# TensorE fill work behind the first group sums and behind the second piece's turn

## What is computed

```python
def ternary_quant(w_fp32, g=GROUP_SIZE):          # GROUP_SIZE = 64
    w = w_fp32.astype(jnp.bfloat16)
    w_g = w.reshape(-1, g)
    scale = jnp.clip(jnp.mean(jnp.abs(w_g), axis=-1, keepdims=True), 1e-08, None)
    q = jnp.clip(jnp.round(w_g / scale), -1, 1)
    w_hat = (q * scale).reshape(w.shape)
    return w + jax.lax.stop_gradient(w_hat - w)
...
x = x + 0.5 * _L0_ffn_ref(_layernorm(x, axis=-1), L0_ffn_w_gate_up, L0_ffn_w_proj)
x = x + _L0_attn_ref(_layernorm(x, axis=-1), L0_attn_w_qkv, L0_attn_w_proj, L0_attn_b_proj)
x = x + 0.5 * _L0_ffn_ref(_layernorm(x, axis=-1), L0_ffn_w_gate_up, L0_ffn_w_proj)
```

## Time and profile before

| | |
|---|---|
| median of 3 runs | 874.05 us |
| the profiled execution's own time | 873.84 us |
| span of its trace | 871.2 us |
| mean granted TensorE clock | 0.996 |
| VectorE busy | 511.7 us (59%) |
| ScalarE busy | 443.0 us (51%) |
| GpSimd busy | 71.5 us (8%) |

### The profile page before, as it was taken

One profiled execution on the slowest core, in us unless ns is written; L12 is line 12 of the kernel. 1 busy time (PEld: TensorE's weight loads), 2 busy tenths in 40 slices (PEclk: granted clock), 3 DMA queues, 4 the chain that ended last, 5 costly groups with the idle time before them and its releaser, 6 DMA issues. The chain is left out here.

```text
span 871.2 us, 13142 instructions
## 1 busy us (share of the span) xinstructions
PE 852.2 (98%) x4932; PEld 413.3 (47%) x4998; DVE 511.7 (59%) x979; ACT 443.0 (51%) x822; POOL 71.5 (8%) x114
## 2 busy tenths in 40 slices
PE   6999999999999989999999999999999999999998
PEld 5544444444444434464646464444444444444445
DVE  7999997824347566657696958433443443432332
ACT  7976667536435555556657463543444344334331
POOL 2211001200010010000000000000000000000000
PEclk9999999999999999999999999999999999999999
DMA  9999508996747679960505062163433343333236
GB/s 262 179 182 125 76 1 169 216 223 185 163 117 149 112 147 196 185 125 1 86 1 86 1 147 97 21 113 73 73 73 72 73 73 73 73 73 61 61 69 136
DMA packets 257486, 94.70 MB, mean 109 GB/s; under 512 B 242832, under 2 KB 245648, under 8 KB 256400
## 3 DMA queue, kind: packets, MB, share of 16 engines
q1 hardware_dynamic: 248448, 73.42, 45.2%
q0 software_dynamic: 5024, 13.11, 6.7%
q10 hardware_dynamic: 3952, 7.34, 2.6%
HBM read 29.62 MB, written 8.39 MB: 44 GB/s over the span
## 5 line engine op out<-in xcount | busy, mean ns | idle before, releaser
L1643 PE MATMUL proj_ps<-down_w,slots 128*128 128x512 bf16 x910 | 202.9, 379 | 1.1 <-issue 0.2
L1172 DVE SCALAR_TENSOR_TENSOR slots<-up_ps,silu 128x512 f32<-128x512 f32 x117 | 80.9, 691 | 179.8 <-PE up_ps L1629 134.2
L1629 PE MATMUL gate_ps<-gu_w,xT 128*128 128x512 bf16 (+1 forms) x762 | 173.1, 368 | 3.1 <-ACT silu L809 2.3
L1629 PE MATMUL up_ps<-gu_w,xT 128*128 128x512 bf16 (+1 forms) x759 | 171.3, 366 | 0.9
L1643 PEld LDWEIGHTS proj_ps<-down_w,slots 128*128 128x128 f16 x928 | 90.7, 98 | 109.9 <-DVE xs L1194 0.8
L809 ACT ACTIVATE silu<-gate_ps 128x512 f32<-128x512 f32 x117 | 68.8, 588 | 142.9 <-PE gate_ps L1629 142.9
L819 ACT ACTIVATE o_buf<-slots 128x512 f32<-128x512 f32 x128 | 80.5, 629 | 113.7 <-DVE slots L1172 113.0
L1629 PEld LDWEIGHTS gate_ps<-gu_w,xT 128*128 128x128 f16 x776 | 74.0, 98 | 88.4 <-ACT silu L809 2.7
L1629 PEld LDWEIGHTS up_ps<-gu_w,xT 128*128 128x128 f16 x776 | 73.7, 98 | 84.4 <-issue 0.8
L1185 DVE SCALAR_TENSOR_TENSOR slots<-slots,inv 128x512 f16<-128x512 f32 x124 | 91.0, 744 | 3.7 <-ACT slots L830 3.6
L830 ACT ACTIVATE slots<-slots,inv 128x512 f16<-128x512 f32 x124 | 86.3, 711 | 11.1 <-POOL inv L709 7.6
(11 more groups left out here) (151 smaller groups left out, 942.4 us busy)
## 6 DMA issues: line engine op xcount, KB each, us to landing
gu_kept<-gu_w POOLq DMA_DIRECT2D x4, 1024.0 KB, 4.7
gu_w<-gu_kept POOLq DMA_DIRECT2D x4, 1024.0 KB, 6.2
out_dram<-xs SPq DMA_DIRECT2D x15, 256.0 KB, 2.4
xs<-in_L_attn_x_dram SPq DMA_DIRECT2D x3, 1024.0 KB, 8.5
aw<-in_L_attn_w_qkv_dram ACTq DMA_DIRECT2D x12, 256.0 KB, 2.9
slots<-in_L_ffn_w_gate_up_dram ACTq DMA_DIRECT2D x5, 512.0 KB, 6.7
aw<-in_L_ffn_w_gate_up_dram POOLq DMA_DIRECT2D x10, 256.0 KB, 5.5
aw<-in_L_ffn_w_proj_dram POOLq DMA_DIRECT2D x8, 256.0 KB, 5.5
```

Of the source, the lines that this page charges most:

```text
L1172: nc.vector.scalar_tensor_tensor(out=h_rows(i, q), in0=bank(up_ps, j), scalar=gu_out(i), in1=silu_rows(j), op0=ALU.mult, op1=ALU.mult).the ...
L1629: mm = nc.tensor.matmul(bank(ps, j)[:, first:first + width], xT(m)[:, t, r, k, :], gu_w[:, q, side, k, first:first + width], start=(k + r ...
L1643: mm = nc.tensor.matmul(proj_ps[:, use % 2, :], h_turned(i)[:, r, j, :], down_w[:, j, :], start=(r + j == 0), stop=(r == 1 and j == HC - 1))
```

## The change

Two of the counts of fill matmuls grow by 18 each. Nothing else differs: no wait, no buffer, no other engine's program.

```diff
-FILL_TURN, FILL_SUMS = (10, 12, 5), (7, 0, 0)
+FILL_TURN, FILL_SUMS = (10, 30, 5), (25, 0, 0)
```

## The result

The changed kernel takes 875.17 us, the median of 15 runs (874.01 to 876.35). The kernel before, in 15 runs, takes 872.97 (871.37 to 875.11). The ratio is 1.002, with a 95% interval of 1.0011 to 1.0028. The profiled execution took 875.39 us, its span is 873.5 us, 2.3 more than before.

What follows compares the result with a forecast made beforehand. TensorE, busy 852.2 of 871.2 us, was taken as the bound, VectorE as pacing the early weight preparation. Blocks and instructions at zero cost and 0.27 us gained took 873.84 to 873.57, said as 873.6 us; range 871.5 to 875.0.

Steps and rivals of the forecast that it cites:

- The bound and the gaps: First 20 us: VectorE paces weight preparation; added blocks fit both TensorE gaps at zero cost and keep the clock up.
- the two holes: TensorE idle 1.53 us ahead of the turn of piece 1 and 1.52 ahead of its group sums; blocks shrink each.
- 0.52 us left in either gap: Behind the 18 added blocks in each gap, 0.52 us should remain before the turn or group sums can start.
- rival C: Second gap's blocks run at the lower clock and delay VectorE by 1.0 us: 874.9 us, chance 0.08.
- What reaches the end: 0.27 us: Means of piece 2 come 0.6 us sooner; VectorE's 0.27 us wait for them goes, and all 0.27 reaches the end.
- The chain: From VectorE at 19.11 through TensorE, ScalarE and the DMA of `x` to TensorE at 50.75: up to 0.27 us sooner.
- Instructions: taken as zero: 72 more instructions on 13142 cost nothing, since no code fetch shows among TensorE's waits; bound 0.15 us.
- Rival A: Start: the clock falls all the same, or the gain is lost on the way: 873.8 us, chance 0.25.
- Rival B: Stall at 320 us: the clock drop behind it, costing 1.6 us, falls away: 872.0 us, chance 0.12.
- D: A clock drop moves from behind the second gap to where TensorE is the bound, costing 1.6 us: 875.4, chance 0.05.

Runs made afterwards that it cites:

- the changed kernel's second trace: The changed kernel measured again with no further edit, beside other runs on the same chip: 874.60 us against 874.06 before, ratio 1.0007.
- the changed kernel with its fetches moved back: 184 semaphore increments in the first four projections added to the changed kernel, 256 instructions in all: 873.14 us, ratio 0.999; second time 873.25, ratio 0.9994.
- 36 increments: The kernel before plus 36 semaphore increments that nobody waits for in the first four projections, no added blocks: 873.24 us against 873.65, ratio 0.9995.
- 88: The kernel before plus 88 semaphore increments that nobody waits for in the first four projections, no added blocks: 876.23 us against 874.06, ratio 1.0020.
- half of the change: The kernel before plus only the 18 more blocks behind the first group sums, none behind the second turn: 873.38 us against 873.94, ratio 0.9996.
- 72 increments: The kernel before plus 72 semaphore increments that nobody waits for in the first four projections, no added blocks: 874.76 us against 873.65, ratio 1.0009.
- wide: The kernel before with 6 blocks in each of the two gaps made 512 columns wide, same instruction count: 874.11 us against 873.65, ratio 1.0003.
- 56: The kernel before plus 56 semaphore increments that nobody waits for in the first four projections, no added blocks: 873.70 us against 874.06, ratio 0.9989.
- 120: The kernel before plus 120 semaphore increments that nobody waits for in the first four projections, no added blocks: 875.68 us against 874.06, ratio 1.0012.

## Why the prediction was wrong

*The bound and the gaps.* Right in their shape: the clock stayed up, the turn of piece 2 took 1.06 us, VectorE's wait went. But the prediction took the fall of the clock for a consequence of the two holes, and four traces with the same second hole have no fall. So that part came true at least partly by luck. In the three traces where it fell, the 36 blocks of the beginning had taken 3.52 to 3.74 us; in the four where it stayed, 4.02. That is a pattern in seven traces, and I did not test it. One part of the sum was off. In the trace of the changed kernel the clock rose late (the first turn takes 1.94 us), so a part of the 25 blocks ran at the lower clock. There were no 0.52 us left in either gap: the group sums at 14.40 start right behind the last block. That is the beginning of rival C. Besides the late tile of `x` it made the means of piece 1 some 0.24 us later on ScalarE, and VectorE's step on them 0.07 us. In the changed kernel's second trace 0.59 and 0.74 us were left.

*What reaches the end: 0.27 us.* Not to be seen, and by the runs probably nothing. Taking all blocks out of the two gaps gives a ratio of 1.0000 (0.9982 to 1.0017), the changed kernel with its fetches moved back 0.999 and 0.9994. In the traces TensorE stands at 54 us anywhere between 1.3 us sooner and 0.8 us later than in the trace of before, and kernels with an unchanged start lie on both sides. 0.27 us would drown in that. The chain was wrong at its last link, too. In the changed kernel's trace VectorE is 0.33 us late from 19 to 50 us and the DMA is issued 0.3 us later than before, yet TensorE's step comes at 50.35, 0.40 us sooner: the transfer took 5.1 us instead of 6.6. In other traces it took up to 7.3. How long it takes, and not when VectorE is ready, decides there.

*Instructions: taken as zero.* This is the step that failed. I looked for the price of longer code among TensorE's waits, found none, and bounded it by 0.15 us. In the stretch of the loss TensorE indeed does not wait for its code. The price is paid by others: by a transpose that runs beside the fetch (on one DMA engine with it, as I read the DMA view), and by all who wait for it. In the changed kernel's trace it was 1.1 us at 309 (310.43 against 309.21, less the 0.09 of before) and 1.0 us more at 343, 2.1 us in all. The trace of before had what was needed: a queue named "instruction" with 39 packets of 16 KB, of which the windows show one each some 28 us in this stage, and a chain of transposes behind which TensorE stalls. The Trainium skill says in "Runtime: NRT & Kernel Launch", section "Instruction fetch mechanics", that code comes in blocks of 16 KiB, 256 instructions, over a DMA queue of the sequencer's own, and that crossing a block's end is mostly hidden. The packets agree in size, and 256 instructions more brought the fetches back to within 2.3 us of their old places. "Hidden" holds in this stretch for TensorE, and not for the transfers beside the fetch.

Perhaps not even for TensorE everywhere. In three traces (36 increments, 88, and half of the change) it stands still for 0.6 to 1.1 us in or just behind a run of 128 matmuls of 33 columns, for nothing that the profile shows ("issue"), and goes on each time 2.4 to 2.6 us behind the start of a fetch. The traces lose 0.8 to 1.3 us there against before, and don't win it back. With 36 increments, where the fetch began at 468.0:

```profile
470.62 0.25 PE L1797 MATMUL proj_ps<-gu_w 128*32 128x33 f32 x2 [0.77 <-issue]
```

That it waits for code there is my reading; no run tests it. If it holds, the prediction's bound of 0.15 us was too small for TensorE's own waits as well.

*Rival A* (nothing happens): with the blocks the clock did not fall in any trace, against its first part; its result, that nothing of the start reaches the end, is what is left when the fetches are moved back.

*Rival B* (the drop of the clock at 321.7 is worth 1.6 us): wrong. Two traces of fourteen have it, that of before and that with 72 increments. With no blocks in the gaps the matmul after the stall starts at 321.71, as before, and runs at full clock:

```profile
321.71 1.90 PE L1629 MATMUL gate_ps<-gu_w,xT 128*128 128x512 bf16 x8 [2.25 <-ACT silu L809]
```

Yet 302 to 361 takes 59.7 us, not 58. The 1.6 us come back as waits of 0.76 us at 341 and 1.25 at 361, where before has none at 341 and 0.51 at 361. My argument was that TensorE is the bound "from there on". It is not before 362 us: the chain of transposes is, and TensorE's clock has slack in it. The kernel with 72 increments has the drop, and takes 61.7 us, as the changed one without it.

*The range.* 875.17 lies 0.17 us above its end. The nearness is chance: rivals C and D, which reach up there, did not happen. A loss that works at a distance was in none of my cases; that the change stays within 0.3% was right.

*Open.* In the changed kernel's first trace 0.5 us more are lost at about 200 us, ahead of a silu. Others lose 0.7 us (no blocks), 1.3 (wide), 2.0 (72), 2.1 (56, a part of it at 224 us) and 2.5 (120) there, and the changed kernel's second trace nothing. The fetches don't explain it: with one at 198.6 us 72 increments lose 2.0, with one at 198.8 us 88 lose nothing. I have no cause for it. The best version measured, the changed kernel with 184 increments, is 0.2 to 0.5 us under before, which is not told apart from no change.

## What to carry to other kernels

An instruction that an engine does for free still lengthens its program, and by the reading above the code is fetched over the same DMA engines as the data. Where the kernel hangs on a transfer that uses all of them, look where the "instruction" packets fall: adding or removing a few dozen instructions anywhere ahead moves them all. And when an edit of this size shows 0.2%, test the length of the code alone, with instructions that do nothing, before explaining the edit. One trace of before is one sample, too: here the clock fell at 15 us in three of seven executions with the same start, so a single trace on each side can't credit an edit with keeping it up.

## What the runs showed of the hardware

A fetch of 16384 bytes took 0.88 to 2.1 us over all traces, where the transpose issued at 305 us took 4.1 to 4.4 us without one in it. The four that fell into that transpose took 0.93, 0.94, 0.93 and 1.56 us (changed kernel twice, 72 and 88 increments), and it landed after 5.3, 5.4, 5.1 and 5.3 us: 1.0 to 1.3 us later than the 4.1 of before. With 256 instructions more ahead of them, the fetches of this stage were back within 2.3 us of their old places. One or two semaphore increments before a matmul of 0.216 us cost TensorE nothing up to 184 in 128 matmuls; two before each took the four projections from 27.63 to 36.09 us.
